# Attention and feed-forward kernel on one Trainium2 core: two more tiles of the probabilities product in three rounded terms, seeds copied straight from PSUM, one row maximum placed elsewhere

## The reference

```
kv = context @ Wkv;  k, v = split(kv);  q = layernorm(x) @ Wq          # heads: 16 x 64
dots = einsum('bhnd,bhmd->bhnm', q, k) * SCALE
dots = dots - (1.0 - mask)[:, None, :, None] * 1000000.0
attn = softmax(dots, axis=-1)
x = x + einsum('bhnm,bhmd->bhnd', attn, v) -> (b, n, h*d) @ Wout + bout
x = x + gelu(layernorm(x) @ w1[expert] + b1[expert]) @ w2[expert] + b2[expert]
```

## Time and profile before

| | us |
|---|---|
| three runs | 374.39, 374.76 (median), 376.75 |
| the profiled execution, as timed | 374.87 |
| its span, first to last instruction | 373.0 |

### The profile page before, as it was taken

The page is one execution under the profiler, slowest core; times in us unless marked ns, Lnnn a source line. Parts: engine busy times, 40 slices in busy tenths (PEclk is TensorE's granted clock), DMA queues, the critical chain, the costliest instruction groups (busy, mean ns, idle before and its releaser), DMA issues.

```text
span 373.0 us, 5778 instructions
## 1 busy us (share of the span) xinstructions
PE 363.0 (97%) x1713; PEld 278.7 (75%) x1713; DVE 279.3 (75%) x458; ACT 255.1 (68%) x335; POOL 116.1 (31%) x125
## 2 busy tenths in 40 slices
PE   6899999999999999999999999999999999999996
PEld 6767777777777887777777877777777877687755
DVE  4888677978797669878797669878797669454863
ACT  3556576697769576697679476697579467796621
POOL 1610573245324430145324440255224440022000
PEclk9999999999999999999999999999999999999998
DMA  7686268329932854339932764349933752438400
GB/s 239 216 195 176 54 129 199 85 83 168 201 94 82 150 98 134 82 104 235 233 88 86 144 113 117 84 117 235 222 86 100 129 108 40 119 68 156 74 2 6
DMA packets 30622, 47.10 MB, mean 126 GB/s; under 512 B 2011, under 2 KB 21371, under 8 KB 30608
## 3 DMA queue, kind: packets, MB, share of 16 engines
q0 software_dynamic: 9936, 27.40, 37.6%
q1 hardware_dynamic: 20672, 19.52, 17.5%
HBM read 24.59 MB, written 0.23 MB: 67 GB/s over the span
## 4 chain that ended last, share of the span: by engine, by line
PE 85%; DVE 10%; issue 2%; ACT 1%; DMA 1%; SPq 0%; DVEq 0%; ACTq 0%
PE ps_s L444 29%; PE ps_a L484 23%; PE ps_x L500 10%; PE ps_a L477 9%; PE ps_x L533 3%; PE ps_a L421 2%; PE ps_x L553 2%; PE ps_x L458 1%; DVE shift_diag L930 1%; DVE ex_sum L900 1%; DMA ex_all<-in_wk_t 1%; PE ps_x L562 1%; DVE chunk_max L919 1%; DVE ex_lo L915 1%; PE ps_x L530 1%
## 5 line engine op out<-in xcount | busy, mean ns | idle before, releaser
L919 DVE TENSOR_REDUCE chunk_max<-ps_x 128x1 f32<-128x500 f32 x168 | 111.1, 677 | 31.9 <-PE ps_x L500 28.8
L708 ACT ACTIVATE ex_all<-ps_s 125x896 f32<-125x896 f32 x95 | 87.1, 917 | 44.1 <-PE ps_s L444 42.7
L484 PE MATMUL ps_a<-ex_all,ctx_sb 125*128 125x448 f32 x248 | 110.9, 541 | 0.0
L726 ACT COPY ps_s<-shift_row 125x896 f32<-125x896 f32 x94 | 85.7, 911 | 12.2 <-DVE shift_row L1057 9.7
L500 PE MATMUL ps_x<-ctxt_hi,qk_hi 128*128 128x500 f32 x168 | 80.7, 484 | 1.1 <-DVE chunk_max L919 0.9
L1234 POOL DMA_DIRECT2D ex_all<-ex_all x48 | 42.2, 878 | 115.9 <-ACT ex_all L708 111.6
L444 PE MATMUL ps_s<-qk_hi,ctxt_hi 128*125 128x448 f32 x192 | 76.3, 479 | 0.0
L484 PEld LDWEIGHTS ps_a<-ex_all,ctx_sb 125*128 125x128 f32 x248 | 46.3, 190 | 17.1 <-issue 12.7
L444 PE MATMUL ps_s<-qk_hi,ctxt_lo 128*125 128x448 f32 x192 | 54.9, 367 | 0.0
L444 PE MATMUL ps_s<-qk_lo,ctxt_hi 128*125 128x448 f32 x192 | 54.7, 366 | 0.0
L444 PEld LDWEIGHTS ps_s<-qk_hi,ctxt_hi 128*125 128x125 f32 x192 | 35.9, 187 | 24.4 <-issue 23.3
(11 more groups left out here) (110 smaller groups left out, 382.1 us busy)
## 6 DMA issues: line engine op xcount, KB each, us to landing
ex_all<-ex_all POOLq DMA_DIRECT2D x48, 448.0 KB, 4.6
ctxt_raw<-in_ctx_t SPq DMA_DIRECT2D x8, 750.0 KB, 6.5
ctx_sb<-in_ctx SPq DMA_DIRECT2D x8, 750.0 KB
ctxt_hi<-in_ctx_t POOLq DMA_DIRECT2D x21, 250.0 KB, 3.1
w_sb<-in_w SPq DMA_DIRECT2D x4, 512.0 KB, 5.0
w_sb<-in_w SPq DMA_DIRECT2D x8, 256.0 KB, 6.6
ex_all<-in_wq_t SPq DMA_DIRECT2D x2, 256.0 KB, 3.8
ex_all<-in_wk_t SPq DMA_DIRECT2D x2, 256.0 KB, 4.8
```

What stands on the lines that cost most here:

```text
L484: mm = nc.tensor.matmul(ps_a[:, c, 0:CH], ctx_sb[0:MT, u, t, :], ex(t)[0:MT, c * CH:(c + 1) * CH], start=(slot == 0), stop=(slot == TM - 1))
L708: nc.scalar.activation(half(ex(t)[0:MT, :]), src, ACT.Exp, scale=SCALE).then_inc(ex_ready, 1)
L726: nc.scalar.copy(ps_s[0:MT, t % 2, :, 0:CH], half(shift_row[0:MT, b.parity, :])).then_inc(seeded, 1)
L919: nc.vector.tensor_reduce(chunk_max[:, k, t:t + 1], filled()[:, 0:MC], AX.X, ALU.max).then_inc(job_free, 1)
```

## The change

- `SPLIT` becomes [0, 2, 4, 6, 8, 10]. Tile 0 gets `ex_hi` on ACT in step 0 and `ex_lo` on DVE at (1, 1); tile 10 gets `ex_hi` in step 10, ahead of the next seed, and `ex_lo` at (11, 0). Slots 10 and 11 change places: tile 11 first, then tile 10. In batch 7 tile 10 stays plain. `ctx_hi` and `ctx_lo` hold six tiles instead of four.
- Row maxima: (2, 2) goes; in even batches (8, 1) comes, ahead of the hidden layer, in odd ones (4, 0).
- The shift products stand behind the whole of slot 8, at (10, 3). ACT copies them from `ps_x` into `ps_s` (`first_seed`), and then into `shift_row`, which frees both banks at once; the two DVE copies of `shift_copies` go, but for batch 0's own.
- `sum_high_part` moves from the end of step 0 to step 1, ahead of `att_out`; `sum_hi` shares memory with `shift_diag`. Two additions of DVE move by a step or a place. Batch 0's `ctx_hi` is made ahead of its iteration.

```diff
-    SPLIT = [2, 4, 6, 8]
-    PV_ORDER = [0, 1, 2, 3, 5, 4, 7, 6, 9, 8, 10, 11]
+    SPLIT = [0, 2, 4, 6, 8, 10]
+    PV_ORDER = [0, 1, 2, 3, 5, 4, 7, 6, 9, 8, 11, 10]
     MAX_AT = [
-        [(1, 0), (1, 1), (1, 2), (2, 0), (2, 1), (2, 2), (4, 0), (4, 1), (4, 2), (5, 0), (5, 1), (5, 2),
-         (6, 0), (6, 1), (6, 2), (7, 0), (7, 1), (7, 2), (8, 0), (8, 2), (9, 0)],
-        [(1, 0), (1, 1), (1, 2), (2, 0), (2, 1), (2, 2), (4, 1), (4, 2), (5, 0), (5, 1), (5, 2),
+        [(1, 0), (1, 1), (1, 2), (2, 0), (2, 1), (4, 0), (4, 1), (4, 2), (5, 0), (5, 1), (5, 2),
+         (6, 0), (6, 1), (6, 2), (7, 0), (7, 1), (7, 2), (8, 0), (8, 1), (8, 2), (9, 0)],
+        [(1, 0), (1, 1), (1, 2), (2, 0), (2, 1), (4, 0), (4, 1), (4, 2), (5, 0), (5, 1), (5, 2),
          (6, 0), (6, 1), (6, 2), (7, 0), (7, 1), (7, 2), (8, 0), (8, 1), (8, 2), (9, 0)],
     ]
-    FIRST_SHIFT_AT, SHIFT_AT = (0, 1), (TM - 2, 2)
-    ADD_AT = {(10, 2): (0,), (11, 0): (1, 2)}
-    ADD_LATE = (3, 4)
+    FIRST_SHIFT_AT, SHIFT_AT = (0, 1), (TM - 2, 3)
+    ADD_AT = {(10, 2): (0,), (11, 1): (1, 2)}
+    ADD_LATE = {(0, 0): (3, 4)}
+    LOW_AT = [(t + 1, 1) for t in SPLIT[:-1]] + [(11, 0)]
...
+            def first_seed(b):
+                act.wait_ge(job_ready, jobs.value())
+                act.wait_ge(ex_ready, b.at(TM, -1))
+                nc.scalar.copy(ps_s[0:MT, 0, :, 0:CH], ps_x[0:MT, :, 0:CH]).then_inc(seeded, 1)
+                nc.scalar.copy(half(shift_row[:, b.parity, :]), ps_x[:, :, 0:CH]).then_inc(job_free, 2)
...
                     if t == 1 and b.off > 0:
+                        sum_high_part(b.later(-1))
                         att_out(b.later(-1))
+                    if prepare and t == TM - 2:
+                        ex_high_part(b, SPLITS - 1)
...
                         if t + 2 == TM:
                             jobs.n = FIRST_JOBS if first else jobs.n + 2
+                            first_seed(b.later(1))
+                        else:
                             act.wait_ge(job_free, jobs.value())
-                        seed(b.later(1), t + 2 - TM)
-                    if t == 0 and b.off > 0:
-                        sum_high_part(b.later(-1))
...
                     if prepare and at == SHIFT_AT:
-                        shift_copies(b.later(1))
+                        jobs.n += 2
```

More of the change, by code:

```diff
@@ L185, in xattn_ffn @@
         inv_sum = sb("inv_sum", [P, Q])
-        sum_hi = sb("sum_hi", [P, Q], F32R)
+        sum_hi = shift_diag[:, :, :].rearrange("p t q -> p (t q)")
         sum_lo = sb("sum_lo", [P, Q], F32R)
@@ L277, in read_by, with buffer_free @@
             return PV_ORDER.index(t) + 1
+        def buffer_free(n):
+            return read_by(SPLIT[n - 2]) if n >= 2 else read_by(SPLIT[SPLITS - 2 + n]) - TM
         def summed(t):
@@ L477, in probs_ctx @@
                             mm = nc.tensor.matmul(ps_a[:, c, 0:CH], a[0:MT, u, n, :], e[0:MT, n % 2, c * CH:(c + 1) * CH],
-                                                  start=False, stop=False)
+                                                  start=(slot == 0 and term == 0), stop=(slot == TM - 1 and term == 2))
                     mm.then_inc(pv_done, 1)
@@ L566, in shift_jobs @@
             def shift_jobs():
-                for c in range(2):
+                for _ in range(2):
+                    c = jobs.n % 2
                     shift_rows(job()[:, 0:CH], P, c, start=True).then_inc(job_ready, 1)
@@ L603, in iteration @@
                         jobs_at((t, 2))
+                    jobs_at((t, 3))
             def xnt_job(first, end, step):
@@ L713, in ex_high_part @@
                 act.wait_ge(ex_ready, b.at(TM, t + 1))
-                if n >= 2:
-                    act.wait_ge(pv_done, b.at(TM, read_by(SPLIT[n - 2])))
+                wait(act, pv_done, b.at(TM, buffer_free(n)))
                 nc.scalar.copy(ex_hi[0:MT, n % 2, :], ex(t)[0:MT, :]).then_inc(ex_hi_ready, 1)
@@ L807, in iteration @@
                             jobs.n = FIRST_JOBS if first else jobs.n + 2
+                            first_seed(b.later(1))
+                        else:
                             act.wait_ge(job_free, jobs.value())
-                        seed(b.later(1), t + 2 - TM)
-                    if t == 0 and b.off > 0:
-                        sum_high_part(b.later(-1))
-                    if t == 1 and first:
-                        ctx_high_part(b)
+                            seed(b.later(1), 1)
                     if t == CTX_HI_AT and prepare:
                         ctx_high_part(b.later(1))
-                    if t in SPLIT:
+                    if t in SPLIT[:-1]:
                         ex_high_part(b, SPLIT.index(t))
@@ L849, in _ @@
             for h in range(HEADS):
+                if h == HEADS - BEHIND:
+                    ctx_high_part(Batch(None, 0))
                 drain_later_queries(h)
@@ L913, in ex_low_part @@
                 dve.wait_ge(ex_hi_ready, b.at(SPLITS, n + 1))
-                wait(dve, pv_done, b.at(TM, read_by(SPLIT[n - 2]) if n >= 2 else read_by(SPLIT[n - 2]) - TM))
+                wait(dve, pv_done, b.at(TM, buffer_free(n)))
                 nc.vector.tensor_tensor(ex_lo[0:MT, n % 2, :], ex(SPLIT[n])[0:MT, :], ex_hi[0:MT, n % 2, :].bitcast(F32),
@@ L1053, in shift_copies @@
             def shift_copies(b):
-                wait(dve, seeded, b.at(TM, -TM - 2))
-                for c in range(2):
+                for _ in range(2):
+                    c = jobs.n % 2
                     nc.vector.tensor_copy(shift_row[:, b.parity, c * CH:(c + 1) * CH], filled()[:, 0:CH]).then_inc(job_free, 1)
@@ L1109, in add @@
                 def add(at):
-                    if at == (0, 0) and b.off > 0:
-                        for n in ADD_LATE:
-                            add_to_sum(b.later(-1), n)
+                    for n in ADD_LATE.get(at, ()) if b.off > 0 else ():
+                        add_to_sum(b.later(-1), n)
                     for n in (ADD_AT if prepare else LAST_ADD_AT).get(at, ()):
                         add_to_sum(b, n)
-                    if (at[0] - 1, at[1]) in [(t, 1) for t in SPLIT]:
-                        ex_low_part(b, SPLIT.index(at[0] - 1))
+                    if at in LOW_AT and (prepare or LOW_AT.index(at) < SPLITS - 1):
+                        ex_low_part(b, LOW_AT.index(at))
                 for t in range(TM):
@@ L1126, in iteration @@
                     drain((t, 2))
+                    drain((t, 3))
                     between((t, 3))
@@ L1244, in iteration @@
                 for t in range(TM):
-                    if b.i is None and b.off == 0 and t == 2:
+                    if b.i is None and b.off == 0 and t == 0:
+                        pool.wait_ge(shift_ready, 1)
                         ctx_low_part(b)
@@ L1260, in iteration @@
                     if prepare and t == 6:
-                        pool.wait_ge(ex_lo_ready, b.at(SPLITS, 2))
+                        pool.wait_ge(ex_lo_ready, b.at(SPLITS, 3))
                         ctxt_lo_chunk(b.later(1), 1)
@@ L1265, in iteration @@
                     if prepare and t == 8:
-                        pool.wait_ge(ex_lo_ready, b.at(SPLITS, 3))
+                        pool.wait_ge(ex_lo_ready, b.at(SPLITS, 4))
                         ctxt_lo_chunk(b.later(1), 2)
```

## The result

The changed kernel takes 377.1 us (median of 20 runs, 376.5 to 380.0), the kernel before, run beside it, 374.9 (20 runs, 374.4 to 378.6): a ratio of 1.0058, with an interval of 1.0043 to 1.0073. Forecast were 374.3, and faster by 0.5. The profiled execution has a span of 374.8 us against 373.0, with the same mean granted clock, 0.995.

The account below looks back on a forecast made before the run. TensorE's own work was taken as the bound. Batch 0 +0.79, odd batches -1.0, even -0.3 and batch 7 0 made -0.5 us: execution 374.87 to 374.4, median 374.3, range 371.0 to 377.0 for 8 in 10.

Parts of the forecast that it names:

- The sum: All batches: +0.79 in batch 0, -1.0 in three odd, -0.3 in three even, 0 in batch 7; together -0.5 us.
- the term for tile 4: Tile 4, all batches but 0 and 7: PE waits 0.44 for the third maximum's bank; even -0.17, odd +0.17 us.
- batch 0: First batch: PE's (2, 1) comes 1.07 late behind ex_lo of tile 0; with -0.28 for tile 0, +0.79 us.
- tile 8: Even batches: maximum (8, 1) adds 0.225 and the hidden layer waits 0.40 for (8, 0); +0.625 us each.
- This chain: ACT's att_out to the logarithms, VectorE's refinement, tile 4's maxima: hangs on slot 11, only 0.19 shorter, logarithms 0.16 sooner.
- the gain on tile 0: Tile 0 from 1.51 to 1.23 us on PE, 0.28 less; gone in odd and even batches, held by the logarithm chain.
- The end of the batch: Even: shift wait of 0.53 goes, output layer waits 0.27 for ACT's second copy, -0.26 us; odd: shift -0.23.
- Batch 7: Last batch: att_out and slot 0 come 0.53 late, slots 11 and 0 gain 0.56; 0 us.
- everything is hidden: Rival, chance 0.16: the forecast waits don't come, through slack in PE's queue or the drains; -6.5 us, 368.3, half of them 371.
- all five waits: New PE waits: tile 4 0.44, hidden layer 0.40, output layer 0.27, batch 0 1.07, batch 7 0.53 us.
- The seed path: Rival, chance 0.10: ACT's PSUM to PSUM copy costs 1.82, delaying out_job and exp(11); 3.6 us in all, 377.9.
- within 1%: Whole kernel's time changes by no more than 1%, 3.7 us: chance 0.76, against faster 0.16 and slower 0.08.

Follow-up runs that it names:

- experiment 1: The changed kernel with GpSimd's ctxt_lo held back until VectorE's ex_lo of tile 2 is made: 374.2 us, ratio 0.9971 to the kernel before.
- 3: The kernel before with an extra 310-column subtraction on GpSimd ahead of qk_lo, so ctxt_lo begins before ex_lo of tile 2: 376.3 us, ratio 1.0027.
- Experiment 7: The changed kernel with the row maxima where they were before and tile 0 plain again, tile 10 still in three terms: 371.9 us, ratio 0.9912.
- versions 5 to 8: Four follow-up kernels: 5, 373.0 us; the kernel before with the shift part of the change alone, 372.6 us; Experiment 7, 371.9 us; 8, 371.8 us.
- 5: The changed kernel with the old row maxima and GpSimd's ctxt_lo held back behind ex_lo of tile 2: 373.0 us, ratio 0.9937.
- 8: As 5, but in batch 0 VectorE makes ex_lo of tile 0 behind the maximum (1, 2): 371.8 us, ratio 0.9906.

## Why the prediction was wrong

The sum said -0.5 us in the batches and the trace says +1.95; the medians differ by +2.2. Of the 2.45 that are missing, 2.1 are in the term for tile 4: 3 x 0.42 in the even batches, 2 x 0.48 - 0.12 in the odd ones. 0.33 are in batch 0, 0.2 in tile 8, and the rest gives 0.1 back.

**The step that failed** is tile 4. "This chain hangs on slot 11, which M moves with, and nothing in the change shortens it but that 0.19": nothing shortens it, but something lengthens it. The step counted VectorE's L963 from ACT's logarithms alone and took ex_lo of tile 2, ahead of it on VectorE, at the 1.09 of the earlier trace rows. It had priced ctx_lo on GpSimd by GpSimd's free time and had not followed the other instructions of GpSimd, whose start hangs on sum_lo, which the change had moved. Against experiment 1, ex_lo takes 0.85 more in batch 4 and 0.95 more in batch 3; less the 0.25 for which L963 waits anyway there, and 0.08 by which it begins ahead of the end of ex_lo's record, that is what L963 comes late by (0.52 and 0.62, from the batch's first exponential), and tile 5 of PE with it (0.51 and 0.60). Experiment 1 takes it away without touching VectorE, ACT or PE, and 3 brings it about in the kernel before; between them they show the cause from both sides. The text did say that each 0.1 in that chain is worth 0.6 us, and gave it no chance of its own.

**Without the overlap the tile 4 term holds.** Experiment 1 has -0.23 in the odd batches for a forecast of -0.11, -0.54 in the even ones for -0.45. The wait of PE before the third maximum is there (0.33 by starts, forecast 0.44), as is the reason for it: the gain on tile 0 goes to the logarithm chain. Experiment 7 shows this from the other side: with tile 0 plain no loop batch is slower by more than 0.07.

**Batch 0** cost 1.12 and not 0.79. The mechanism was right. The size was off by what looks like the same cause, though no version removed it alone: ex_lo of tile 0 took 1.47 there, 0.38 too long, while GpSimd made qk_lo. By starts (2, 1) is 1.43 late (36.95 against 35.11 + 0.41), forecast 1.07.

**Tile 8** was +0.69 for +0.63. The hidden layer, listed at 222.16, follows (8, 1) at 221.55 by 0.61 where 0.225 would do: it waits 0.38 for (8, 0), forecast 0.40.

```profile
221.55 0.39 PE L505 MATMUL ps_x<-ctxt_hi,qk_hi 128*128 128x500 f32 x1
222.16 1.99 PE L558 MATMUL ps_x<-z_t,w_sb 128*128 128x64 f32 x16 [0.23 <-DVE chunk_max L935]
```

**The end of the batch** was right: the shift products follow slot 8 without a wait (-0.22 in an odd batch, forecast -0.23), and the output layer waits for ACT's second copy, 233.03 + 0.91 = 233.94, and starts at 233.99: -0.30 for -0.26. The copy PSUM to PSUM, which no row of before had, took 0.894 on average over 7, for the 0.91 taken between bounds of 0.7 and 1.82.

```profile
233.03 0.91 ACT L739 COPY shift_row<-ps_x 128x896 f32<-128x896 f32 x1
...
233.99 1.09 PE L567 MATMUL ps_x<-w_sb,w_qk 128*64 128x128 f32 x16 [0.18 <-ACT shift_row L739]
```

**Batch 7** was right (-0.04 for 0): slot 0 comes 0.59 late (326.20 against 325.20 + 0.41), forecast 0.53. A three-term tile took 1.23: slot 0 of batch 0 begins at 37.18, the next scores at 38.41. By the four passes of the Trainium skill ("FP8 and Floating Point Precision", TensorE Precision Notes) it would have been an estimated 1.13; the trace does not agree.

**The rivals.** That everything is hidden did not come: all five waits came, at tile 4 in every loop batch, ahead of the hidden layer and of the output layer, in batch 0 and in batch 7. The seed path did not become the bound. The side of slower was given to the one mechanism that the copy's price would decide, and 0.08 in all to slower by over 1%; the change ended at 0.6% slower, inside "within 1%", which had 0.76. The range ended at 377.0, 0.1 short. A rival in which VectorE's ex_lo waits out GpSimd's 1.26 was missing. From the rows of before: at most 1.26 more, less the 0.45 for which L947 waits anyway, is 0.8 a batch and 4.9 in six, 379.2; with the 0.95 that was found it is 0.5 a batch, 377.3.

**What stays open:** why the medians of versions 5 to 8 differ by less, or by more, than their batches do (1.2 us of median between 5 and 8, 0.5 in the batches, the rest in the start and the tail). And GpSimd's ctxt_lo in batch 1 began behind ex_lo and not ahead of it, by 0.11 us; that it starts later there because the batch before is batch 0 was not tried.
